# A shorter inverse root on VectorE, and expert slices moved around the projections of a two-layer block

## What is computed

```python
x = x + layernorm(attn(layernorm(x)))         # window of 250 keys, rope, out_proj
x = x + layernorm(ffn(layernorm(x)))
# ffn(src): full attention with compressed k and v and rope, times Wo
#   x  = rmsnorm(src + sa, norm1_w)
#   shared = swiglu(x @ W_shared_in) @ W_shared_out
#   h      = swiglu(x @ W1_shared)
#   routed = sum over 8 experts of (h @ W2_experts[e]) * w[:, e]   # top 2 of one group
#   return rmsnorm(x + shared + routed, norm2_w)
```

## Time and profile before

| | before |
|---|---|
| median of 3 runs | 2038.05 us (2035.23 to 2042.69) |
| profiled execution | 2036.16 us, span 2034.4 us |
| PE, DVE, ACT, POOL busy | 92%, 68%, 40%, 19% of the span |
| mean granted clock of PE | 0.949 of full speed |

### The profile page before, as it was taken

How to read it: one execution, slowest core, us unless ns; L and a number is a source line. 1 busy time by engine, 2 the same in 40 slices (tenths; PEclk the granted TensorE clock), 3 DMA queues, 4 the chain that set the end, 5 groups by cost and what they waited for, 6 DMA issues and landing times.

```text
span 2034.4 us, 28180 instructions
## 1 busy us (share of the span) xinstructions
PE 1877.2 (92%) x9244; PEld 1045.4 (51%) x9244; DVE 1388.0 (68%) x4368; ACT 807.9 (40%) x1730; POOL 377.6 (19%) x669
## 2 busy tenths in 40 slices
PE   6968899999999999999999999999999999999987
PEld 4343454636455363644537355553646546374556
DVE  6457474875868567685877857686686857768367
ACT  3433534254333634335352453325433363533410
POOL 1336023101221013200241012310122101410010
PEclk8576899999999999999999999899999999999999
DMA  3026002201031100401022010221003110220420
GB/s 107 2 76 235 22 22 84 83 7 48 23 135 42 43 21 19 165 7 53 22 95 83 2 53 23 98 80 37 17 22 135 43 43 32 78 90 2 176 83 11
DMA packets 31297, 123.06 MB, mean 60 GB/s; under 512 B 5424, under 2 KB 18352, under 8 KB 26544
## 3 DMA queue, kind: packets, MB, share of 16 engines
q1 hardware_dynamic: 28624, 105.54, 14.2%
q0 software_dynamic: 2528, 15.73, 2.0%
HBM read 101.33 MB, written 18.87 MB: 59 GB/s over the span
## 4 chain that ended last, share of the span: by engine, by line
PE 65%; DVE 25%; issue 5%; ACT 3%; DMA 1%; POOL 0%; SPq 0%; DVEq 0%; ACTq 0%; POOLq 0%
PE fb L843 11%; PE ot L782 11%; PE sm L741 8%; DVE negmax L1196 6%; PE fb L821 5%; PE st L768 5%; PE st L709 3%; PE fb L817 3%; DVE sm L1193 2%; PE fb L839 2%; PE st L725 2%; DVE acc L1394 2%; PE sm L768 2%; PE dn L709 2%; PE dn L794 2%
## 5 line engine op out<-in xcount | busy, mean ns | idle before, releaser
L621 ACT ACTIVATE probs<-st 128x512 f32<-128x512 f32 (+3 forms) x832 | 396.6, 507 | 429.7 <-PE st L768 425.5
L843 PE MATMUL fb<-w_r,h_r 128*128 128x512 f32 x1344 | 395.2, 423 | 0.0
L741 PE MATMUL sm<-k_t,q_t 48*128 48x512 f32 (+3 forms) x864 | 324.3, 457 | 52.7 <-DVE negmax L1193 20.7
L1196 DVE TENSOR_REDUCE negmax<-sm 128x1 f32<-128x512 f32 x416 | 269.4, 685 | 83.9 <-PE sm L741 82.6
L768 PE MATMUL st<-q_t,k_t 64*128 64x512 f32 (+3 forms) x832 | 306.8, 462 | 20.4 <-ACT probs L621 19.6
L741 PEld LDWEIGHTS sm<-k_t,q_t 48*128 48x128 f32 x864 | 147.3, 197 | 311.1 <-DVE negmax L1193 135.8
L843 PEld LDWEIGHTS fb<-w_r,h_r 128*128 128x128 f32 x1344 | 236.5, 192 | 93.8 <-issue 56.2
L1193 DVE CUSTOM_DVE_ANT_0 sm<-sm,mask_qk 128x384 f32<-128x384 f32 (+1 forms) x448 | 203.6, 468 | 109.6 <-PE sm L741 106.8
L782 PE MATMUL ot<-probs,v_s 128*32 128x512 f32 (+3 forms) x2048 | 260.9, 543 | 2.6 <-POOL probs L496 2.6
L455 POOL TENSOR_TENSOR stack<-rot,stack 128x256 fp32r<-128x256 f32 x64 | 50.0, 782 | 1005.2 <-ACT stack L557 1005.2
L768 PEld LDWEIGHTS st<-q_t,k_t 64*128 64x128 f32 x832 | 136.4, 197 | 117.4 <-ACT probs L621 83.6
(11 more groups left out here) (210 smaller groups left out, 2661.4 us busy)
## 6 DMA issues: line engine op xcount, KB each, us to landing
w_r<-w_parts SPq DMA_DIRECT2D x30, 2048.0 KB, 7.9
wup_r<-wup_parts SPq DMA_DIRECT2D x32, 512.0 KB, 4.3
w_parts<-w_r POOLq DMA_DIRECT2D x4, 2048.0 KB, 9.2
x_s<-in_L_attn_query SPq DMA_DIRECT2D x8, 512.0 KB, 4.8
q_t<-rot_b SPq DMA_DIRECT2D x256, 4.0 KB
x_kept<-o_s SPq DMA_DIRECT2D x8, 512.0 KB, 3.0
h_s<-in_L_ffn_W_experts POOLq DMA_DIRECT2D x8, 512.0 KB, 5.1
xa<-x_kept SPq DMA_DIRECT2D x8, 512.0 KB, 3.2
```

The lines of the kernel that those rows point to most:

```text
L621: nc.scalar.activation(probs[:, n % PSLOTS, 0:hi - lo], score_bank(m)[:, 0:hi - lo], ACT.Exp, scale=float(D) ** -0.5).then_inc(s_ex, 1)
L741: mm(max_bank(w, a)[:, 0:hi - lo], q_t[r:r + MROW, b, t * P:(t + 1) * P], k_t[r:r + MROW, b, lo:hi], start=True, stop=True).then_inc(s_sm, 1)
L843: last = mm(fb[q % 2][:, :], h_r[:, h, m, rows], w2_r[:, k % 2, w, m, :], start=(m == 0 and n == 0), stop=(m == NH - 1 and n == 2))
L1196: return v.tensor_reduce(negmax[:, g % 2, n // GH, c:c + 1], max_bank(g * UNITS + n, a)[:, 0:hi - lo], AX.X, ALU.max, negate=True).then_in ...
```

## The change

`inverse_root` has 8 instructions: the guess takes one (the bits times -0.5 plus the constant), then one step of third order takes four and a Newton step three. Half of set 1 goes behind the first out-projection; set 16 is cut 1, 2, 1 around the second one's transposes; DVE reads set 1 and set 2 within the first scale and set 5 behind the centring; the two `unread` products on `dn` go; three constants of the step tables move.

```diff
--- before.py
+++ after.py
@@ -48,8 +48,10 @@
 QUIET_OUT = [g * UNITS + n for g in range(NGR) for n in ((2, 8, 12) if g else (4, 8, 12))]
 HIDDEN_AT = spread(8 * NH - len(QUIET), 4 - LEAD, 3) + QUIET
 OUT_FIRST, OUT_BESIDE = range(2, 7), range(9, 16)
-OUT_END = {0: (((0, 0), (0, 1)), ((0, 2), (0, 3)), ((1, 0), (1, 1), (1, 2), (1, 3))),
-           1: (((16, 0), (16, 1)), ((16, 2), (16, 3)), ())}
+OUT_END = {0: (((0, 0), (0, 1)), ((0, 2), (0, 3)), ((1, 0), (1, 1))),
+           1: (((16, 0),), ((16, 1), (16, 2)), ((16, 3),))}
+
+OUT_PROJECTED = ((1, 2), (1, 3))
 
 OUT_ROWS, OUT_FIRST_HEADS, OUT_LEAD = 17, 18, 19
 
@@ -64,10 +66,10 @@
 GATES_FROM = LOGITS_AT[-1] + 2
 GATE_EXPS_AT = (GATES_FROM + 6, GATES_FROM + 12)
 RING = 2
-SOURCE_FIRST, SOURCE_STEPS = 18, 2
+SOURCE_FIRST, SOURCE_STEPS = 15, 2
 STEPS_AT_LAST, STEPS_BESIDE_LAST = 9, 9
 SOURCE_FROM = 36
-FINISH_FROM, FINISH_TWO_FROM = 20, 47
+FINISH_FROM, FINISH_TWO_FROM = 21, 45
 
 
 LEAD_WIDE, TAIL_WIDE = (range(2 * GH, LEAD - GH), range(0, LEAD - GH)), ALL - LEAD + 4
@@ -76,6 +78,8 @@
 
 AHEAD = (2, 1)
 RSQRT_MAGIC = float(0x5F3759DF)
+
+THIRD = 0.375
 
 
 def build(nc, x, in_w, out_w, wq, wkc, wvc, wk, wv, wo, w_si, w_so, w1, w2, wgg, weg,
@@ -152,7 +156,6 @@
         mv = sb("mv", [P, NT, 2])
         spare = sb("spare", [P, 1])
         var = sb("var", [P, NT])
-        bits = sb("bits", [P, NT], I32)
         rstd = sb("rstd", [P, NT])
         nt1 = sb("nt1", [P, NT])
         nt2 = sb("nt2", [P, NT])
@@ -994,9 +997,10 @@
                 attention(i, f, e, 0)
                 project_attention(i, f, 0, wout_t)
                 if f is not None:
+                    for q, m in OUT_PROJECTED:
+                        expert_out(f, q, m)
                     for q in OUT_FIRST:
                         out_rows(f, q)
-                    unread(dn, 2)
                 pe.wait_ge(s_xn, i + 1)
                 transpose_rows(xn, pair, s_tp)
                 if f is not None:
@@ -1118,21 +1122,30 @@
             def inverse_root(c):
 
                 settle()
-                signal(v.tensor_scalar(bits[:, c], var[:, c].bitcast(I32), 1, None, ALU.logical_shift_right))
-                yield
-                settle()
-                signal(v.tensor_scalar(rstd[:, c].bitcast(I32), bits[:, c], -1.0, RSQRT_MAGIC, ALU.mult, ALU.add))
-                yield
-                for _ in range(3):
-                    settle()
-                    signal(v.tensor_tensor(nt1[:, c], rstd[:, c], rstd[:, c], ALU.mult))
-                    yield
-                    settle()
-                    signal(v.scalar_tensor_tensor(nt2[:, c], nt1[:, c], -0.5, var[:, c], ALU.mult, ALU.mult))
-                    yield
-                    settle()
-                    signal(v.scalar_tensor_tensor(rstd[:, c], nt2[:, c], 1.5, rstd[:, c], ALU.add, ALU.mult))
-                    yield
+                signal(v.tensor_scalar(rstd[:, c].bitcast(I32), var[:, c].bitcast(I32), -0.5, RSQRT_MAGIC,
+                                       ALU.mult, ALU.add))
+                yield
+                settle()
+                signal(v.tensor_tensor(nt1[:, c], rstd[:, c], rstd[:, c], ALU.mult))
+                yield
+                settle()
+                signal(v.scalar_tensor_tensor(nt2[:, c], nt1[:, c], -1.0, var[:, c], ALU.mult, ALU.mult))
+                yield
+                settle()
+                signal(v.scalar_tensor_tensor(nt1[:, c], nt2[:, c], 10.0 / 3.0, nt2[:, c], ALU.add, ALU.mult))
+                yield
+                settle()
+                signal(v.scalar_tensor_tensor(rstd[:, c], nt1[:, c], 5.0, rstd[:, c], ALU.add, ALU.mult))
+                yield
+                settle()
+                signal(v.tensor_tensor(nt1[:, c], rstd[:, c], rstd[:, c], ALU.mult))
+                yield
+                settle()
+                signal(v.scalar_tensor_tensor(nt2[:, c], nt1[:, c], -0.5 * THIRD ** 3, var[:, c], ALU.mult, ALU.mult))
+                yield
+                settle()
+                signal(v.scalar_tensor_tensor(rstd[:, c], nt2[:, c], 1.5 * THIRD, rstd[:, c], ALU.add, ALU.mult))
+                yield
 
             def layer_scale(c=slice(0, NT)):
                 settle()
@@ -1276,7 +1289,7 @@
                 run(others)
                 run(later)
                 normalise(i, a, NGR - 1)
-                out_now(f, sorted({q for part in OUT_END[a] for q, m in part}))
+                out_now(f, [q for part in OUT_END[a] for q, m in part if m == NH - 1])
 
             def first_source(i):
 
@@ -1512,7 +1525,7 @@
                 run(source)
                 attention(i, f, e, 0, more)
                 run(moments(projected, lambda t: dve.wait_ge(s_pj, i * N_PJ + t // 2 + 1)))
-                weave(layer_scale(), f, OUT_FIRST[0:1])
+                weave(layer_scale(), f, [q for q, m in OUT_PROJECTED if m == NH - 1] + [OUT_FIRST[0]])
                 settle()
                 v.scalar_tensor_tensor(nt1[:, :], mv[:, :, 0], -1.0, rstd[:, :], ALU.mult, ALU.mult).then_inc(s_ctr, 1)
                 out_now(f, OUT_FIRST[1:2])
@@ -1528,12 +1541,11 @@
                 v.memset(spare[:, :], 0.0).then_inc(s_pr, 1)
 
                 run(moments(lambda t: x1[:, t, :]))
-                out_now(f, OUT_FIRST[3:4])
                 run(layer_scale())
                 for t in range(NT):
                     last = centre(xn[:, t, :], x1[:, t, :], t)
                 last.then_inc(s_xn, 1)
-                out_now(f, OUT_FIRST[4:])
+                out_now(f, OUT_FIRST[3:])
                 heads(i, 1, beside_second)
                 attention(i, f, e, 1, more)
                 dve.wait_ge(s_pj, i * N_PJ + 4)
```

## The result

The changed kernel takes 2025.66 us (median of 14 runs, 2011.16 to 2035.10), the kernel before, on the same chip and in turns with it, 2040.47 us (14 runs, 2033.66 to 2049.72). The ratio is 0.9919, 95% interval 0.9896 to 0.9941: faster by 14.8 us where 21 were forecast. Run once more (e5) it gave 0.9925 [0.9899, 0.9951], 2025.62 against 2036.82 us. A ratio here leaves out runs over 1.5% above the fastest of the same kernel, which are one of e5's 12 and five of e7's 12. The profiled execution took 2026.88 us with a span of 2025.2, against 2036.16 and 2034.4 before.

What follows compares the result with a forecast made beforehand. PE held 65% of the chain and DVE 25%, so savings count where DVE stands between PE's work. Terms 10.9 + 4.2 + 1.6 + 1.8 + 0.6 + 2.0 = 21.1 us gave 2016 us, range 2007 to 2027.

Steps and rivals of the forecast that it cites:

- The step, 0.20 us: DVE's scale: each dependent instruction costs 0.20 us, so a root shorter by three saves 0.6 us wherever it runs through.
- The centring, 1.55 us a round: Rounds 1 to 7: read gone between moments and scale, shorter scale; 1.55 us a round, 10.9 us in all.
- set 4 ends where it did: Centring: PE's products up to set 4 are only permuted, so it still ends at 841.2 and DVE waits.
- set 1 is read too late: Rival at the centring: set 3 waits for DVE's read of set 1, 0.4 us a round, time 2019; chance 0.12.
- set 3 waits for DVE: Sign at the centring that the prediction is wrong; a margin of 0.2 us was expected there.
- Second out-projection, 0.7: Rounds 1 to 7: set 16's last slice moves into PE's 0.74 us wait for ACT's copies; 0.7 us a round.
- the heads behind it, 0.24: Next heads: PE's 0.88 us wait for DVE's copy becomes about 0.65; 1.4 us over six heads.
- Round 0, 1.8 us: Round 0, no sets to fill it: 0.6 us at the first source and 1.2 for two scales.
- Behind the last round, 2.0: After round 7: 1.3 gained at the projection, 1.3 lost at the last hidden block, 2.0 gained at the end.
- I leave them as they are, with 5 us either way: PE's clock falls in all rounds: assumed unchanged by the edit, with 5 us allowed either way.
- the clock gives half back: Rival: four rounds each get 2.9 us longer from lost clock, 11.6 us in all, time 2028; chance 0.08.
- The last rival: Centring without the unread products: PE's clock falls, 4.9 us lost a round, 34 us in all, time 2050; chance 0.02.

Runs made afterwards that it cites:

- e7: Changed kernel with one unread product at every second position of both attentions of round 0; 2026.53 us (7 of 12 runs), ratio 0.9961.
- e1: Kernel before with only the shorter inverse root and the three numbers that depend on its length; 2035.23 us, ratio 0.9995.
- e3: Changed kernel with set 5 read ahead of the scale again, as before; 2040.96 us, ratio 1.001.
- e4: Changed kernel with the two unread products on `dn` put back behind set 6; 2022.35 us, ratio 0.9918.
- e12: Changed kernel with the edits of e4 and e6 together; 2028.18 us (12 runs), ratio 0.9953.
- e6: Changed kernel with one unread product at each of two small gaps in the second attention of rounds 1 to 7; 2019.45 us (6 runs), ratio 0.9915.
- e9: The same kernel as e6, run again; 2014.81 us (6 runs), ratio 0.9877.
- e8: Changed kernel with one unread product at every position of both attentions of round 0; 2067.99 us (5 runs), ratio 1.0151.

## Why the prediction was right, and where it was off

The forecast (2016 us, 2007 to 2027, faster 0.90) has the sign, and its mechanism stands in rounds 1 to 7 and at the end. The time, 2025.66, is 1.3 us inside the range, and the gain is 14.8 us of the 21.1 summed. That it fell inside is in part luck: the clock, of which the forecast could say nothing, took 6 to 7 us.

- **The step, 0.20 us.** Right: 1.78 us for nine instructions, and e1's centring 0.61 us shorter.
- **The centring, 1.55 us a round.** From the transposes of `o_s` to those of `xn` it was 20.12 us (828.61 to 848.73), now 18.80 (823.14 to 841.94), so 1.32. The argument held that set 4 pins DVE and that the scale and the read behind it count (e3: 0.95 for the read). What failed is "set 4 ends where it did". From the first projection to the first products of set 4's kind it is 7.77 us (824.97 to 832.74), before 6.72 (831.27 to 837.99), 1.05 more where 0.86 were moved, so sets 4 to 6 end 0.19 us late. Half of this is in the projection itself, 3.72 us in place of 3.62: its weights waited for ACT's second copy, which ends at 824.91, so the start that the copy "just allows" is late. The other half is behind it: from the first of the sets' products to set 4's kind it is 4.21 us (828.53 to 832.74) in place of 3.27, 0.94 more for the 0.86, and there the loads of set 3 waited 0.22 us for DVE's read of set 1. That is the rival "set 1 is read too late", and the forecast's own sign of being wrong, "set 3 waits for DVE"; but it costs 0.08 us a round and not 0.4.
- **Second out-projection, 0.7, and the heads behind it, 0.24.** The second attention's stage, which holds the slice, is 0.65 us shorter. In the heads PE waited 0.88 us for a copy of DVE; after, it waits 0.49 there and, one copy further on, 0.28 for ACT's, 0.77 in place of the 0.65 counted:

```profile
971.44 0.51 PE L728 MATMUL sm<-ident_r,stack 128*128 128x128 f32 x4 [0.49 <-DVE q_t L1195]
...
972.90 0.53 PE L728 MATMUL sm<-ident_r,stack 128*128 128x128 f32 x4 [0.28 <-ACT q_t L560]
```

The first stage as a whole gives 1.19 us for the 0.86 + 0.24 + 0.1 = 1.20 of the sum.
- **Round 0, 1.8 us.** Not confirmed. The first transposes start at 13.49 us in place of 14.15, 0.66 for the first source's 0.6, and the centring takes 17.22 us in place of 18.40, for the 1.2 of two scales. But most of round 0 runs at half clock, and its stages move with the places of the full clock: in e5, the same kernel as after, the transposes start at 14.47 us and the centring takes 18.66. And the round as a whole is no shorter. Its first stage is 0.65 us shorter (97.28 to 96.63), its second attention 2.9 longer (107.68 to 110.53) at the same clock of 0.73, though no edit touches it, and round 1 begins at 241.43 us in place of 241.06. In e5 that second attention takes 109.36 us; why it differs I did not try.
- **Behind the last round, 2.0.** The end is as priced: from the start of the last set's products 15.04 us (2019.36 to 2034.4) before and 13.07 after, 1.97. The other half was wrong by two prices. The last hidden block was to be waited for 7.3 us, and was for 5.17:

```profile
1955.38 2.23 DVE L1167 TENSOR_SCALAR acc<-acc,mv,rstd 128x256 f32<-128x256 f32 x3
1957.65 1.43 DVE L1481 TENSOR_TENSOR acc<-acc,xa 128x256 f32<-128x256 f32 x4
1959.71 0.69 DVE L1428 SCALAR_TENSOR_TENSOR sg<-sg,sm 128x512 f32<-128x512 f32 x1
```

```profile
1960.45 9.97 PE L842 MATMUL fb<-wso_s,h_s 128*128 128x256 f32 x32 [5.17 <-DVE sg L1428]
```

That is DVE's timeline, then PE's, behind the last round of after. The four adds stand ahead of the block, as the step count said, but take 1.43 us, not the 2.49 of the earlier trace rows, which they took beside a subtraction on POOL. That is 1.06 us of the 2.1. Another 0.98 is an instruction of `finish` that ran beside such a subtraction (from 1954.67) in the kernel before:

```profile
1954.75 1.46 DVE L1158 SCALAR_TENSOR_TENSOR acc<-acc,rstd,norm_w 128x256 f32<-128x256 f32 x1
```

In after all four of this kind take 0.48 us each. From the last second out-projection to the end it is 113.68 us in place of 118.25. Of these 4.57 us at most 1.46 are a smaller loss of clock (window length times the missing clock of 0.06 and 0.07, 6.82 and 8.28), so 3.1 or more are left, and the sum has 1.3 for this window (its 2.0 less round 7's slice, which the second attention's window holds).

**The sum at equal clock:** seven rounds of 2.33, 16.3, where the terms make 18.0; round 0, -0.4 as traced, for 1.8; the end without its clock share, 3.1, for 1.3. Together it is 19.0 us, where the sum said 21.1; over all runs it is 19.6 (20.6 with a slope of 1500). So the 21.1 is near because a gain at the end that was priced too low makes up for much of what the rounds and round 0 fell short by.

**The step that failed** is "I leave them as they are, with 5 us either way". The clock fell by 0.0048 in the mean of 26 runs against 86, 6 to 7 us given back. It is the rival "the clock gives half back" at half its price, and it came by no mechanism that I named. It also moved the rounds: those of after, 1 to 6, take 234.3 to 242.0 us in the traced execution, where 236.5 to 239 were forecast. The last rival, a clock lost at the centring's gap, is refuted at its place (1.00 there in rounds 1 to 7 of every trace, with the products or without). Whether their removal costs clock elsewhere is open: with them back the clock rose by 0.0040 in e4, but e1 lost 0.0039 without removing them, and e12, which has them and e6's fills, has 0.9446 against e6's and e9's 0.9477 and 0.9520. The Trainium skill ("TensorE: Matmul & The Clock Gate", Part 1, the HAM clock gate) says that only activity keeps the clock released. Of the gaps in the second attention the counts agree (3 of 28 rounds with the fill against 33 of 70). The fall at 1231 in e5, with PE busy for 14 us before it, does not agree, and there the measurement decides. What stays open is what sets the mean clock of a program: kernels that differ by a few products or steps have means from 0.938 to 0.9575.

## What to carry to other kernels

Where the clock varies, compare windows between the same two instructions at the same granted clock: they repeat to 0.03 us in a short stage and 0.3 in the longest, and priced a step of 0.2 us, while one run of this kernel moves by 7 us for 0.005 of clock. When a read in the middle of a latency chain pins it, look at what runs behind that read and not ahead of it: of the 0.86 us by which the projection came earlier nothing was left at set 4, and the 0.92 and 0.6 us behind it reached PE but for 0.2. A duration from a row is one of its neighbours too: ask whether another engine ran beside it.

## What the hardware showed that I had not expected

- The clock halved after PE had been busy for 14 us, in a stretch with products of 10 columns (13.6 us at half, e5). With two groups of these products doubled no such fall was seen (0 of 12 rounds, against 15 of 72), which is too few to call it their doing.
- A POOL `TENSOR_TENSOR` stretches some of what DVE runs beside it. POOL and DVE behind the last round, after:

```profile
1952.02 1.26 POOL L487 TENSOR_TENSOR h_r<-sg,h_r 128x512 fp32r<-128x512 f32 x1 [2.82 <-ACT h_r L560]
```

```profile
1952.18 1.12 DVE L1141 TENSOR_TENSOR nt<-rstd 128x4 f32<-128x4 f32 x1
1953.34 0.16 DVE L1144 SCALAR_TENSOR_TENSOR nt<-nt,var 128x4 f32<-128x4 f32 x1
```

A DVE instruction over four columns takes 1.12 us, until POOL is done, and the next of the same size 0.16. The adds of 1.43 us took 2.49 in the same way before. The Trainium skill ("GPSIMD Engine Reference", section 1, Specifications) says that POOL shares its SBUF interfaces with DVE, in contention with DVE instructions that have two SBUF inputs or run in a 2-port mode. The trace agrees: the stretched ones here have two SBUF inputs, while four BN_STATS with one input, started beside such a POOL instruction at 1947.93, took their usual 1.41 us.
- To hold the clock with added products costs more than it brings where PE is busy most of the time anyway: 0.93 and 0.97 of clock in place of 0.66 and 0.73, and stages longer by 28.8 and 18.8 us (e8).
